# Attention steps on TensorE: both products for the maxima in a row, the side product after them

## What is computed

```python
x = x + 0.5 * ffn(layernorm(x))          # 8 experts of 256 -> 1024 -> 256, and one dense
x = x + attention(layernorm(x))          # 8 sequences of 1024 tokens, 16 heads of 16
x = x + 0.5 * ffn(layernorm(x))
...
xd = (x @ W_down).reshape(b, t, h, s)
keys, queries, values = (einsum('bthk,hik->bthi', xd, w) ...)
dot = einsum('bqhs,bkhs->bhqk', queries, keys)
attn = softmax(dot, axis=-1)
out = einsum('bhqk,bkhs->bqhs', attn, values).reshape(b, t, e) @ W_unify + b_unify
```

## Time and profile before

| what | value |
|---|---|
| median of 3 runs | 2892.79 us (2887.39 to 2898.54) |
| profiled execution, its own time | 2896.95 us |
| its span | 2895.2 us |
| granted TensorE clock over the span | 0.964 |
| PE, DVE, ACT busy | 2705.7, 2145.9, 1821.3 us |

### The profile page before, as it was taken

The page is one execution under the profiler, slowest core; times in us unless marked ns, Lnnn a source line. Parts: engine busy times, 40 slices in busy tenths (PEclk is TensorE's granted clock), DMA queues, the critical chain, the costliest instruction groups (busy, mean ns, idle before and its releaser), DMA issues. The chain is left out here.

```text
span 2895.2 us, 48611 instructions
## 1 busy us (share of the span) xinstructions
PE 2705.7 (93%) x17009; PEld 1644.3 (57%) x17009; DVE 2145.9 (74%) x3552; ACT 1821.3 (63%) x3409; POOL 599.8 (21%) x562
## 2 busy tenths in 40 slices
PE   5899999867999999999999999999999589999997
PEld 3799999863334334333343343433433368999886
DVE  6555456747899898998998988989895665554574
ACT  5344556632777776777777767777777444444564
POOL 3355114521100100101001001010000235521353
PEclk9899999986999999999999999999999789999998
DMA  5211113414123132131231321312310512111341
GB/s 172 66 44 44 58 45 106 133 60 75 30 50 75 33 61 54 39 62 36 50 75 33 60 55 39 62 37 50 60 28 5 173 30 80 44 44 45 102 133 63
DMA packets 164529, 181.69 MB, mean 63 GB/s; under 512 B 38472, under 2 KB 133904, under 8 KB 164368
## 3 DMA queue, kind: packets, MB, share of 16 engines
q1 hardware_dynamic: 156176, 169.03, 24.0%
q0 software_dynamic: 8192, 10.57, 1.2%
HBM read 97.51 MB, written 31.54 MB: 45 GB/s over the span
## 5 line engine op out<-in xcount | busy, mean ns | idle before, releaser
L1457 ACT ACTIVATE at_ex<-at_pd 128x512 f32<-128x512 f32 x2048 | 1084.7, 600 | 383.7 <-PE at_pd L1360 379.2
L1521 DVE TENSOR_REDUCE at_mxc<-at_pb 128x2 f32<-128x1024 f32 x1024 | 1219.0, 1219 | 120.8 <-PE at_pb L1349 113.8
L768 DVE TENSOR_TENSOR f_ml_hl<-f_ml_h,f_ml_hh 128x512 fp32r<-128x512 f32 (+1 forms) x384 | 287.8, 751 | 422.7 <-ACT f_ml_hh L844 421.5
L1360 PE MATMUL at_pd<-at_qa,at_ka 50*128 50x512 f32 x2048 | 583.6, 469 | 3.9 <-ACT at_ex L1457 3.2
L1360 PEld LDWEIGHTS at_pd<-at_qa,at_ka 50*128 50x128 f32 x2048 | 266.6, 185 | 538.4 <-issue 349.2
L1369 PE MATMUL at_po<-at_ex,at_va 128*32 128x512 f32 x4096 | 548.8, 608 | 0.2 <-ACT at_ex L1457 0.2
L841 ACT ACTIVATE f_ml_h<-f_ml_pL,b1T 128x512 f32<-128x512 f32 (+1 forms) x384 | 243.8, 635 | 457.9 <-PE f_ml_pL L895 446.3
L1349 PE MATMUL at_pb<-at_ka,at_qa 48*128 48x512 f32 x2048 | 433.1, 450 | 24.7 <-DVE at_mxc L1521 16.5
L910 PE MATMUL f_ml_pA<-f_wh,f_ml_hh 128*128 128x256 f32 (+1 forms) x1408 | 410.4, 291 | 3.7 <-DVE f_ml_hl L768 3.7
L912 PE MATMUL f_ml_pA<-f_wl,f_ml_hh 128*128 128x256 f32 (+1 forms) x1408 | 402.5, 286 | 0.0
L913 PE MATMUL f_ml_pA<-f_wh,f_ml_hl 128*128 128x256 f32 (+1 forms) x1408 | 402.5, 286 | 0.0
(11 more groups left out here) (128 smaller groups left out, 2636.6 us busy)
## 6 DMA issues: line engine op xcount, KB each, us to landing
f_wraw<-in_L_ffn_w SPq DMA_DIRECT2D x128, 256.0 KB, 2.8
at_qa<-at_parts SPq DMA_DIRECT2D x384, 64.0 KB, 2.4
at_ka<-at_parts SPq DMA_DIRECT2D x384, 64.0 KB, 2.4
f_ro_xr<-in_L_attn_x SPq DMA_DIRECT2D x16, 512.0 KB, 3.9
f_ml_xr<-in_L_attn_x SPq DMA_DIRECT2D x16, 512.0 KB, 4.2
x<-f_ml_yo SPq DMA_DIRECT2D x16, 512.0 KB, 4.0
at_xr<-x SPq DMA_DIRECT2D x16, 512.0 KB, 5.1
at_xres<-x SPq DMA_DIRECT2D x8, 1024.0 KB
```

Source lines behind the costliest of these rows:

```text
L768: eng.tensor_tensor(hl[h % RING][:, 0:w], h32[h % 2][:, 0:w], hh[h % RING][:, 0:w].bitcast(F32), ALU.subtract).then_inc(s_lo.sem, 1)
L1360: eng.matmul(pd[n % RING][:, :], ka[g][rows, p, kt * P:(kt + 1) * P], qa[g][rows, qh, p, :], start=True, stop=True).then_inc(s_full.sem, 1)
L1457: eng.activation(ex[t % 2][:, j, :], pd[n % RING][:, :], ACT.Exp).then_inc(s_free[n % RING].sem, 1)
L1521: eng.tensor_reduce(mxc[:, t // NT, kh, t % NT::NT], pb[kh][:, :].rearrange("p (e k) -> p e k", e=2), AX.X, ALU.max, negate=True).then_inc ...
```

## The change

TensorE's list for a step makes both pairs for the maxima one behind the other, and the side product after them. Before, the side product stood between them. The lists of all other engines stay as they are; so do all instructions, tiles and semaphores. In steps without a side product nothing changes.

```diff
@@ class Do: step (TensorE)
                     for j in range(2 if tiles else 0):
                         for_exp(self.ring, *coming, j, tiles[j])
-                    if ahead:
-                        for_max(*ahead, 0)
+                    for kh in range(2 if ahead else 0):
+                        for_max(*ahead, kh)
                     if a:
                         side_product(self.ring, a)
-                    if ahead:
-                        for_max(*ahead, 1)
                     for j in range(2, GH if tiles else 2):
                         for_exp(self.ring, *coming, j, tiles[j])
                     times_v(self.ring, b, par, g, t, done)
```

## The result

| | before | after |
|---|---|---|
| median | 2895.66 us (4 runs, 2887.39 to 2900.82) | 2927.03 us (4 runs, 2925.79 to 2929.88) |
| profiled execution, its own time | 2896.95 us | 2927.00 us |
| its span | 2895.2 us | 2925.2 us |

The changed kernel is slower by a ratio of 1.0121, 95% interval 1.0104 to 1.0137, which is 30 to 40 us. It was forecast at 2932, between 2914 and 2950, for a rise of 38.7; the medians give 31.4.

What follows compares the result with a forecast made beforehand. TensorE was taken to bound the attention, with VectorE 90% busy behind it. Terms of 13.5+15.9+6.5+1.4+1.4 = 38.7 us, added to 2892.8, gave 2932, range 2914 to 2950.

Steps and rivals of the forecast that it cites:

- the loop through the first exponential: Plain steps: first L1360, exponential, fourth L1360, products with V set the 2.62 us; the 0.28 wait costs nothing.
- TensorE's own account of the change: TensorE's reordered list in side steps: nothing added, side product entered and left once as before, so zero cost.
- "f": Side product of four transposes right behind VectorE's copy of the V products; 63 such steps lengthen, 13.5 us.
- The lost cover: Pair 1's wait for VectorE's reduction lay under the side product; now all behind it waits, 38.7 us, chance 0.80.
- the walk: Step-by-step timing of the attention from fixed constants; in the old order it gives 193.6 us a sequence, trace 194.0.
- "qk": Longer side product, four steps in a row: new loop through ScalarE's copy, L1572 and reduction, 4.09 a step, 15.9 us.
- g=0, t = 2 to 6: Steps where VectorE also makes the next sequence's statistics and normalizations: +0.93, seven times, 6.5 us.
- "u" and "xd" elsewhere: Long side products outside the statistics stretch: +0.07 to +0.11 in steps that pay, 1.4 us for each kind.
- The upper bound of the forecast: Total if every reduction ends 0.1 later after the step's start, so more side steps pay 0.1 more: +50 us.
- No change, and the price of the shape changes with it: Rival, chance 0.09: reductions are out of the way, only equal TensorE work in another order is left; 2893, within 5.
- Faster by the 0.76: Rival, chance 0.04: the 0.76 before pair 1's load in long side steps is a true wait, won back; 2866.
- Lateness that spreads to all transposes: Rival, chance 0.07: lateness carries over to every run of transposes, 86 steps paying 0.2 to 0.3; 2950 to 2957.

Runs made afterwards that it cites:

- The experiment on VectorE's order: Changed kernel, with VectorE making reduction kh=1 ahead of L1572 in the 28 "qk" steps: 2923.50 us, ratio 1.0096 to the kernel before.
- the third order: Side product ahead of both pairs for the maxima on TensorE, against the kernel before: 2955.81 us against 2891.55, ratio 1.0215.

## Why the prediction was right, and where it was off

- What bounds the kernel. Right: plain steps are unchanged with the same 0.28 of wait; the loop through the first exponential sets them.
- TensorE's own account of the change, zero. Right, and shown: with halved reductions the new row runs 3.09 in an "f" step, side load at T+0.90 (T+0.89 worked out); and in the changed kernel the "v" steps, where VectorE is early, last 3.09 as before.
- The lost cover as the cause. Shown: halving the reductions takes the loss from 5.2 to 0.5 us a sequence. The times L at which the reduction ends after T, read in the changed kernel, are those of the walk: 0.78 in the ordinary "f" (0.79 to 0.81 forecast), 1.08 in the one behind "qk" (1.10), 1.05, 1.04, 0.92 and 1.28 in g=0, t = 2 to 5 (1.06, 1.06, 0.92, 1.32).
- "f": 0.20 forecast for the ordinary one, 0.18 measured; 0.50 forecast behind "qk", 0.47; 13.5 forecast, 10.4 counted against a trace whose own "f" steps are not all at 3.10 (1.3 of the difference is the slow stretch told below, the rest 0.02 to 0.03 a step).
- "qk": 3.52 and three times 4.09 forecast, 3.55, 4.19, 4.01, 4.10 measured; 15.9 us forecast, 16.1 measured. The loop's 4.09 stands in the rows to the hundredth, and 4.10 is the mean of the last three steps. The experiment on VectorE's order shows that it goes through L1572's place. The Trainium skill (TensorE: Matmul & The Clock Gate, Architectural detail) has VectorE take its queue strictly in order; the rows agree, for the reduction, whose pair was loaded at 1579.10, started only at 1581.92, behind L1570.
- g=0, t = 2 to 6: 3.55, 3.55, 2.62, 5.14, 4.31 forecast (19.17), 3.55, 3.54, 2.64, 5.12, 4.33 in the sequence at 1508.73 (19.18). Wrong is how often: it was priced seven times, 6.5 us, but VectorE makes statistics only where a sequence follows. The last sequence has "aT" and "u" and no statistics, its two "aT" last 3.10, and it loses 0.2 in this stretch and not 0.93.
- "u" and "xd" elsewhere +0.10 to +0.12 in the first of a pair, as forecast, and +0.10 in the second "u" of g=3 (0.07 forecast). The upper bound of the forecast counted 44 first "u" and "xd" of their pairs; there are 29.
- The sum. Over the stage the steps sum to +35.1 against 38.7, and the total to 31.4; the interval of the ratio reaches 39.7, so the two are not told apart. In a middle sequence the forecast's terms add up to 5.25, and its steps lose 5.1 to 5.2. The first and the last sequence fall further short of their terms: without the clock's share, told next, the first loses 3.6 against 4.3, the last 1.4 against 2.8, which is the stretch without statistics (0.7), the "f" at g=1, t=9, which has no "qk" ahead of it there and costs 0.18 and not the 0.50 counted, and the steps behind g=3, t=2, where no maxima are left to make and the new order changes nothing (0.4). Two further differences between the profiled executions have nothing to do with the order. They are in the windows of TensorE's clock, of before and then of after, at the last "f" of the last sequence and at the first steps:

```profile
2216.00:2228.00 12.00, 11.29 (x44) 3.34 (x40) 1.37 (x3) 6.50 (x13) 0.00 (x0) 0.57 0.00 0
```

```profile
710.00:719.00 9.00, 9.00 (x38) 3.69 (x36) 7.56 (x19) 4.34 (x8) 1.02 (x1) 0.50 0.24 37
2252.00:2264.00 12.00, 10.91 (x64) 3.55 (x59) 1.38 (x3) 9.48 (x19) 0.00 (x0) 1.00 0.00 0
```

The third column from the right is the granted clock. Before had 0.57 for some 12 us near the end of the stage (steps of 3.50, 4.06 and 4.41), the same place had 1.00 after; after had two first steps at 0.50 (4.07 each in place of 2.61). The first takes 3.7 us off the measured difference, the second adds 2.9: without both the steps would sum to about +36. They go with the execution and not with the order: of the ten profiled executions of this case seven have first steps of 4.07, and four, the kernel before among them, have several slow steps near the last "f". What remains of the 31.4 against 38.7 lies in the run to run spread and ahead of the first and behind the last of these steps, where the profiled execution of after came out 5 us shorter (first T 712.54 and 710.46; from the T of g=3, t=13 in the last sequence to the end 658.2 and 655.2). Its cause stays open.
- Rivals. No change, and the price of the shape changes with it: refuted by the measurement. Faster by the 0.76: refuted, no "xd" step got shorter, neither in the changed kernel (4.35 and 4.24 for 4.25) nor with "xT", "xd" and "v" alone in new order. Lateness that spreads to all transposes: not seen, "v" steps stay at 3.09; only the "aT" of g=0 pay, and only where VectorE has statistics to make beside them.

## What to carry to other kernels

When an engine's list is reordered, the sum of its own work is the smallest part of the account; ask what the moved item was covering. A wait that shows 0.28 us in steps where it is free is a warning for each step in which it would be first in line. Write down when the other engine's release falls relative to the step (here 0.5 to 1.3 us) and how late it may come before the step grows (here 1.2 before; after, by the forecast's sum, 0.61 in a step with transposes and 0.42 in a longer one): the excess, summed over the steps, gave this change to within a few microseconds. Engines that work through their lists in order and wait on each other across a step, here pair 1, side product, copy, L1572, reduction, pair 1, form a loop whose length is a step's length; look for it wherever an item is moved ahead of the work that feeds the other queue.

## What the runs showed of the hardware

A small VectorE operation of 0.17 us took 1.08 us in the rows of the third order above (L1532, 128x16, from 1381.36 to 1382.44) beside a GpSimd operation of 128x512 that ran from 1381.13 to 1382.41: it ended 0.03 us after GpSimd's had. It happens in the kernel before, too, at another line:

```profile
1546.08 1.29 POOL L1665 TENSOR_TENSOR at_parts<-at_xn,at_parts 128x512 fp32r<-128x512 f32 x1
1546.43 0.97 DVE L1528 TENSOR_TENSOR at_nm<-at_mxc 128x16 f32<-128x16 f32 x1
```

No run was made for this alone, but the traces hold both cases many times. In the kernel before, L1528 runs 63 times in the attention: the 7 that met such a GpSimd operation took 0.97, the 56 others 0.17 to 0.18. In the third order it is 7 of L1532 at 1.08 to 1.09, and 55 at 0.16 to 0.17. The reductions beside such GpSimd operations keep their 1.22 us. The Trainium skill (SBUF — State Buffer, Terms and "SBUF: two separate sides") has VectorE and GpSimd lock a shared pair of ports for a whole instruction, and names among the VectorE operations that need it, against a GpSimd operation that reads SBUF, those with two SBUF inputs; both lines have two SBUF inputs, and the reduction reads PSUM, so the rows agree. The traces hold one more case: in the old order with halved reductions a cast with one SBUF input met the GpSimd operation, all 7 times at 1.28 to 1.29 in place of 0.17 to 0.18.

```profile
762.35 1.28 POOL L1665 TENSOR_TENSOR at_parts<-at_xn,at_parts 128x512 fp32r<-128x512 f32 x1
762.37 1.29 DVE L1530 CAST at_mparts<-at_nm 128x16 fp32r<-128x16 f32 x1
```

In the kernel before, the long L1528 was hidden in a step in which VectorE was early; in the third order L1532 lay in front of a waiting TensorE and is part of a step 0.9 us longer than walked. In the changed kernel neither of the two lines (L1526 and L1532 there) met a GpSimd operation (all 0.16 to 0.18), so it has no part in the loss.
